# A two-layer decoder on one core: the score bias of the second cross-attention moved between engines, its outputs packed two heads to a slot, and the opening reordered

## The reference

```python
x = x + L0_attn(layernorm(x), ...)     # gated linear attention, cumulative sums over tokens
x = x + L0_xattn(layernorm(x), ctx)    # softmax cross-attention, keys beyond a length masked
x = x + L0_ffn(layernorm(x), ...)      # two rounds of routed experts, top 2 of 8
x = x + L1_attn(layernorm(x), ...)     # state-space scan, 16 states
x = x + L1_xattn(layernorm(x), ctx, fside, mask)   # softmax cross-attention with a bias
x = x + L1_ffn(layernorm(x), ...)      # quantised feed-forward, 128 -> 512 -> 128
```

```python
q = (query @ Wq.T + bq) * DH ** -0.5;  k = key @ Wk.T + bk;  v = value @ Wv.T + bv
scores = q @ k.T + attn_mask           # attn_mask (256, 256), the same for every batch and head
scores = where(key_padding_mask, -inf, scores)
out = softmax(scores) @ v              # then @ Wo.T + bo
```

## Time and profile before

| | us |
|---|---|
| median of 3 runs | 555.47 (551.81 to 556.1) |
| the profiled execution | 552.34 |
| its span in the profile | 550.6 |

### The profile page before, as it was taken

How to read it: one execution, slowest core, us unless ns; L and a number is a source line. 1 busy time by engine, 2 the same in 40 slices (tenths; PEclk the granted TensorE clock), 3 DMA queues, 4 the chain that set the end, 5 groups by cost and what they waited for, 6 DMA issues and landing times.

```text
span 550.6 us, 9218 instructions
## 1 busy us (share of the span) xinstructions
PE 469.6 (85%) x3087; PEld 276.5 (50%) x3095; DVE 440.8 (80%) x1164; ACT 279.0 (51%) x524; POOL 209.9 (38%) x190
## 2 busy tenths in 40 slices
PE   7789899999998989899989736545679999999866
PEld 6345666666555656566555302212224656666423
DVE  7798866677488557375875999999997789999897
ACT  3840356555544234354433546555530477777675
POOL 8834000000000403341701058999990245554061
PEclk9999999999999999999999956898789999999999
DMA  5510170000010211421200000000001000000001
GB/s 150 146 43 1 59 210 2 1 2 1 2 48 1 87 32 50 130 62 47 74 6 1 2 0 0 0 0 1 1 0 48 2 2 1 2 3 2 1 1 39
DMA packets 25392, 17.34 MB, mean 31 GB/s; under 512 B 2977, under 2 KB 24162, under 8 KB 25346
## 3 DMA queue, kind: packets, MB, share of 16 engines
q1 hardware_dynamic: 24322, 14.65, 9.3%
q0 software_dynamic: 1024, 2.10, 1.3%
HBM read 10.06 MB, written 5.51 MB: 28 GB/s over the span
## 4 chain that ended last, share of the span: by engine, by line
PE 39%; DVE 11%; POOL 11%; issue 5%; ACT 4%; POOLq 0%; DVEq 0%; ACTq 0%
PE PS L1346 7%; PE PS L814 5%; POOL E L2206 5%; PE PS L1460 4%; PE PS L1394 4%; POOL KSA L2198 3%; PE PS L859 3%; PE PS L876 3%; PE PS L1482 2%; POOL OT L2191 2%; PE PS L2085 1%; PE PS L1469 1%; PE PS L356 1%; PE PS L834 1%; PE PS L886 1%
## 5 line engine op out<-in xcount | busy, mean ns | idle before, releaser
L859 PE MATMUL PS<-QM,KP 32*128 32x256 f32 x512 | 91.9, 398 | 1.2 <-ACT E L1047 0.8
L814 PE MATMUL PS<-KP,QP 32*128 32x256 f32 x512 | 78.0, 400 | 0.5 <-ACT QP L1025 0.5
L1047 ACT ACTIVATE E<-PS 128x512 f32<-128x512 f32 x100 | 56.1, 595 | 35.0 <-PE PS L859 24.3
L2662 POOL DMA_INDIRECT sorted<-VA,slot_of x16 | 15.7, 980 | 145.3 <-DVE expert_at L1750 128.3
L859 PEld LDWEIGHTS PS<-QM,KP 32*128 32x128 f32 x512 | 60.6, 184 | 6.2 <-issue 4.8
L814 PEld LDWEIGHTS PS<-KP,QP 32*128 32x128 f32 x512 | 51.4, 184 | 14.5 <-issue 10.0
L1346 PE MATMUL PS<-XNT,KSA 128*128 128x512 f32 x128 | 58.6, 596 | 0.0
L1123 DVE CUSTOM_DVE_ANT_0 SCR<-PS,KSA 128x256 f32<-128x256 f32 x128 | 47.5, 420 | 9.1 <-PE PS L814 8.3
L356 PE MATMUL PS<-KSA,select 128*128 128x512 bf16 x60 | 23.4, 478 | 36.1 <-ACT KSA L2120 30.4
L1118 DVE TENSOR_REDUCE MXT<-PS 128x2 f32<-128x512 f32 x64 | 41.1, 686 | 14.4 <-PE PS L814 14.3
L2635 POOL TENSOR_TENSOR VA<-VA,KSA 128x512 f32<-128x512 f32 x28 | 35.2, 1275 | 37.4 <-ACT VA L1052 37.4
(11 more groups left out here) (343 smaller groups left out, 1033.3 us busy)
## 6 DMA issues: line engine op xcount, KB each, us to landing
KSA<-in_w SPq DMA_DIRECT2D x2, 1024.0 KB, 6.7
sorted<-zeros SPq DMA_DIRECT2D x2, 960.0 KB, 6.4
answers<-OT SPq DMA_DIRECT2D x14, 128.0 KB, 1.8
KSA<-in_w SPq DMA_DIRECT2D x2, 512.0 KB, 9.2
QP<-sorted SPq DMA_DIRECT2D x4, 256.0 KB, 3.1
QP<-sorted SPq DMA_DIRECT2D x2, 448.0 KB, 4.5
X<-in_x SPq DMA_DIRECT2D x2, 256.0 KB, 3.3
SCR<-in_ctxT SPq DMA_DIRECT2D x1, 512.0 KB, 6.3
```

What stands on the lines that cost most here:

```text
L814: ins = pe.matmul(score_bank(n, i)[:, q * S:(q + 1) * S], QP[rows(i), g, t:t + P], KP[rows(i), g, b * S:(b + 1) * S], start=True, stop=Tru ...
L859: ins = pe.matmul(o[:, kt * S:(kt + 1) * S], KP[rows(i), g, t:t + P], QM[rows(i), g, b * S:(b + 1) * S], start=True, stop=True, skip_group ...
L1047: act.activation(slot(m, j), drain_bank(L, m, j), ACT.Exp).then_inc(sig("exps"), 1)
```

## The change

It has three parts.

1. **Bias.** `LOOSE` becomes (0, 1): POOL biases items 0 and 1, DVE items 2 and 3. DVE's two adds of a quad are made together, after both items are computed: one instruction of 1024 columns where the two banks are neighbours, which holds for nine of the 14 quads (1, 2, 4, 5, 7, 8, 10, 11, 13), and two of 512 columns one after the other in the other five. ACT's late exponentials come in the quad's own round.
2. **Packed outputs, in both cross-attentions.** Quads 0 and 1 of a batch accumulate into the same columns, and so do quads 2 and 3: the value tile holds the odd quads' values 9 columns further on, with zeros elsewhere. So ACT's copy to OT has 256 columns in place of 512, and PE turns two blocks in place of four. The output weights of both cross-attentions are loaded in 16 DMAs in place of two, and the value tile is filled in more and smaller instructions.
3. **Opening.** POOL's fills of the value and query-weight tiles, and one of its mask operations, move from the front to behind the outer products of tiles 3 and 1. The projection of keys for the first cross-attention waits for features of batch 0, and ACT copies it after batch 1 (not batch 0). In `pair` the gate's exponential comes last. `turn_mixed` and `project_mixed` come one tile later on PE, and the gate of batch 3 comes after tile 5 on DVE.

```diff
@@ second cross-attention: who adds the bias
         def vector_bias(L, m, j):
-            return L == 1 and (m >= LOOSE_QUADS or j in (1, 2))
+            return L == 1 and (m >= LOOSE_QUADS or j not in LOOSE)
-        LOOSE = (0, 3)
+        LOOSE = (0, 1)
+        def neighbours(m):
+            return (HG * m + 2) % 3 < 2
...
+            def add_bias_pair(m):
+                dve.wait_ge(sig("shifted_scores"), I0 + HG * (m + 1))
...
+                if neighbours(m):
+                    first = 3 + (HG * m + 2) % 3
+                    o = PS[:, first:first + 2, :]
+                    ins = dve.tensor_tensor(o, o, BIASF.unsqueeze(1).to_broadcast([P, 2, HALF]), ALU.add)
+                else:
+                    for j in (2, 3):
+                        o = weight_bank(m, j)
+                        ins = dve.tensor_tensor(o, o, BIASF, ALU.add)
+                ins.then_inc(sig("biased"), 1)
...
                 for j in range(HG):
+                    if L == 1 and j == 3 and 0 <= k - LAG < LOOSE_QUADS:
+                        add_bias_pair(k - LAG)
                     if k < QUADS:
                         maximum(k, j)
-                    if 0 <= k - LAG < QUADS and vector_bias(L, k - LAG, j):
+                    if LOOSE_QUADS <= k - LAG < QUADS and vector_bias(L, k - LAG, j):
                         add_bias(k - LAG, j)
...
-                    if j == 0 and k > LAG and pool_bias(L, k - LAG - 1, 3):
-                        late_exps(k - LAG - 1, 3)
-                    if j == 1 and pool_bias(L, k - LAG, 0):
-                        late_exps(k - LAG, 0)
+                    if j in (1, 2) and pool_bias(L, k - LAG, j - 1):
+                        late_exps(k - LAG, j - 1)
@@ packed outputs
+                r, x = divmod(g, 2)
...
-                        ins = pe.matmul(bank(6)[rows(i), (g % 2) * S:(g % 2) * S + S], VX[:, QT * b + kt, HG * g + i, :],
-                                        slot(m, j)[:, kt * S:(kt + 1) * S], start=(kt == 0), stop=(kt == QT - 1),
-                                        skip_group_check=True)
+                        ins = pe.matmul(bank(6)[rows(i), r * S:(r + 1) * S], VX[:, QT * b + kt, HG * g + i, :],
+                                        slot(m, j)[:, kt * S:(kt + 1) * S], start=(kt == 0 and x == 0),
+                                        stop=(kt == QT - 1 and x == 1), skip_group_check=True)
...
-                for g in range(NG):
+                for r in range(2):
...
-                act.activation(OT[:, 2 * x:2 * x + 2, b * S:(b + 1) * S], bank(6).rearrange("p (g t) -> p g t", g=2),
-                               ACT.Copy).then_inc(sig("o_taken"), 1)
+                act.activation(OT[:, x, b * S:(b + 1) * S], bank(6)[:, x * S:(x + 1) * S], ACT.Copy)\
+                    .then_inc(sig("o_taken"), 1)
@@ output weights
-            for A in range(3):
-                load(woc[:, A, :], ...)
+            load(woc[:, 0, :], ...)
...
+            for A in (1, 2):
+                for k in range(2 * HG):
+                    r, i = divmod(k, HG)
+                    load(woc[16 * k:16 * k + 16, A, :],
+                         inp["w_out"][A][2 * r:2 * r + 2, 32 * i:32 * i + DH, :], "weights_in")
@@ opening
-            keys_project(pe, 0)
+            pe.wait_ge(sig("features"), 1)
+            pe.wait_ge(sig("self_taken"), 1)
+            keys_project(pe, FEATURE_BANK[0])
...
-                if b >= 2:
-                    read = (1, 3)[b - 2]
-                    pe.wait_ge(sig("features"), read)
-                    pe.wait_ge(sig("self_taken"), read)
+                if b == 2:
+                    pe.wait_ge(sig("keys"), 1)
+                if b == 3:
+                    pe.wait_ge(sig("features"), 3)
+                    pe.wait_ge(sig("self_taken"), 3)
...
-                if j == 4:
+                if j == 5:
                     turn_mixed(pe, 0)
-                if j == 5:
+                if j == 6:
                     project_mixed(pe, 0)
...
                 if b == 0:
                     entry_take(act, 0, 1)
-                    keys_take(act, 0)
                 if b == 1:
+                    keys_take(act, FEATURE_BANK[0])
                     keys_clear(act, range(NG))
...
-                    if b + 2 < B:
-                        feature(b + 2)
+                    if b == 0:
+                        feature(2)
+                    if b == 1:
+                        feature_soft(3)
                 if j == 5:
+                    feature_gate(3)
                     self_residual(dve, 0)
...
+                if j == 1:
+                    pool.tensor_scalar(NEGT, VMASK, -1.0, NEG_X0, ALU.add, ALU.mult).then_inc(sig("neg"), 1)
+                if j == 3:
+                    pool.memset(WP[:, :, :, :], 0.0).then_inc(sig("constants"), 1)
+                    value_frame(pool)
```

More of the change, by code:

```diff
@@ L71, in build @@
                    ("logits", 3): 6}
-        WEIGHTS = 16 * 16
+        WEIGHTS = 16 * 30
         def sig(name):
@@ L439, in context_values, with value_slots, take_values @@
             ins.then_inc(sig("vx_psum"), 1)
-        def take_values(act, dst, first_bank):
+        def value_slots(x):
+            return VX[:, :, :, :].rearrange("p j (r x i) c -> p (j r) x i c", r=2, x=2)[:, :, x, :,
+                                                                                        (DH + 1) * x:(DH + 1) * x + DH]
+        def take_values(act, first_bank):
             for half in range(2):
-                ins = act.activation(dst[:, 4 * half:4 * half + 4, :, 0:DH].rearrange("p j h e -> p (j h) e"),
-                                     bank(first_bank + half).rearrange("p (a e) -> p a e", e=DH), ACT.Copy)
+                src = bank(first_bank + half).rearrange("p (a x i e) -> p a x i e", x=2, i=HG, e=DH)
+                for x in range(2):
+                    ins = act.activation(value_slots(x)[:, 8 * half:8 * half + 8, :, :], src[:, :, x, :, :], ACT.Copy)
             return ins
@@ L463, in context_mask @@
             ch.link(ins)
-            pool.tensor_scalar(NEGT, VMASK, -1.0, NEG_X0, ALU.add, ALU.mult).then_inc(sig("neg"), 1)
             pool.wait_ge(sig("ctx_in"), 16)
@@ L467, in context_mask, with value_frame @@
             pool.tensor_tensor(CTM, CT, VMASK, ALU.mult).then_inc(sig("ctx_masked"), 1)
+        def value_frame(pool):
+            packed = VX[:, :, :, :].rearrange("p j (r x i) c -> p (j r) x i c", r=2, x=2)
+            for n in range(4):
+                js = slice(4 * n, 4 * n + 4)
+                pool.memset(packed[:, js, 0, :, DH + 1:32], 0.0)
+                pool.memset(packed[:, js, 1, :, 0:DH + 1], 0.0)
+                ins = pool.memset(packed[:, js, 1, :, 2 * DH + 2:32], 0.0)
+            ins.then_inc(sig("constants"), 1)
+            pool.memset(packed[:, :, 0, :, DH:DH + 1], 1.0)
+            pool.memset(packed[:, :, 1, :, 2 * DH + 1:2 * DH + 2], 1.0).then_inc(sig("constants"), 1)
         def neg_rows(eng, L):
@@ L612, in feature_soft @@
                 gate = GATE[:, js, :]
-                dve.wait_ge(sig("self_gate"), b + 1)
-                dve.tensor_scalar(gate, gate, 1e18, 1.0, ALU.min, ALU.add).then_inc(sig("gate_den"), 1)
                 dve.wait_ge(sig("self_sp"), b + 1)
@@ L617, in feature_soft @@
                 src = PS[:, FEATURE_BANK[b]:FEATURE_BANK[b] + QT, 0:2 * D]
+                dve.wait_ge(sig("self_taken"), b + 1)
                 dve.scalar_tensor_tensor(f, src, 0.0, f, ALU.max, ALU.add).then_inc(sig("features"), 1)
+                dve.tensor_scalar(gate, gate, 1e18, 1.0, ALU.min, ALU.add).then_inc(sig("gate_den"), 1)
             def feature_gate(b):
@@ L1269, in context_half_vector @@
             dve.wait_ge(sig("context_half"), half + 1)
-            dve.tensor_tensor(VX[:, 4 * half:4 * half + 4, :, 0:DH],
-                              bank(CONTEXT_BANK[half]).rearrange("p (j h e) -> p j h e", j=4, e=DH),
-                              brow[:, :].rearrange("p (h e) -> p h e", e=DH).unsqueeze(1).to_broadcast([P, 4, H, DH]),
-                              ALU.add).then_inc(sig(("half_read", "vx_ready")[half]), 1)
+            src = bank(CONTEXT_BANK[half]).rearrange("p (j r x i e) -> p j r x i e", j=4, r=2, x=2, e=DH)
+            row = brow[:, :].rearrange("p (r x i e) -> p r x i e", r=2, x=2, e=DH)
+            for x in range(2):
+                dst = value_slots(x).rearrange("p (j r) i e -> p j r i e", r=2)[:, 4 * half:4 * half + 4]
+                for r in range(2):
+                    ins = dve.tensor_tensor(dst[:, :, r, :, :], src[:, :, r, x, :, :],
+                                            row[:, r, x, :, :].unsqueeze(1).to_broadcast([P, 4, HG, DH]), ALU.add)
+            ins.then_inc(sig(("half_read", "vx_ready")[half]), 1)
         def tile_bank(i):
```

40 lines of the change are left out of this document (20 added, 20 removed).

## The result

Six runs of the changed kernel have a median of 559.05 us (557.19 to 561.31), six of the kernel before 553.03: a ratio of 1.0109, with a 95% interval of 1.0081 to 1.0137. The change costs 6 us. The forecast was 555.0 and no change; the time lies in its range of 549.5 to 560.5, outside the 552 to 558.5 that it gave for the forecast itself, and on the side it gave 0.16. The profiled execution of the changed kernel took 558.83 us, with a span of 557.1, against 552.34 and 550.6.

The account below looks back on a forecast made before the run. It took a loop of waits through the engines (4.78 us a round) as the bound; -2.6 + 0.2 - 1.8 + 5.9 - 0.4 = +1.3, on the 553.9 average, gave 555 us, range 549.5 to 560.5.

Parts of the forecast that it names:

- The loop through the add of item 2: Second cross-attention: item 2's exponential waits for both adds, lengthening the loop by 0.53 nine times and 0.61 five times; +5.9 us.
- Some of it is absorbed: Second cross-attention: VectorE's own queue covers part of the longer loop, taking 2 us off 7.9.
- Packed outputs: First cross-attention: `turn_out` rounds 0.22 shorter, six rounds and two tail turns, -1.8 us; value copies in four instructions, +0.2.
- The last tail: End of the second cross-attention: packed turns on the path save 0.2, ScalarE's shorter last copy 0.2; -0.4 us.
- The output weights: 16 SyncE loads in place of two cost 9.3 us more, under about 10 us of cover; cost 0.
- The opening: First stage: earlier batch 1 features and later `turn_mixed` bring the last tile's products from 57.66 to 55.1; -2.6 us.
- tile 2's products: Opening: these start at 32.7 and not 33.46, with batch 2's features at 27.3 on ScalarE; -0.8 us.
- The 1.80 at 47.09: Opening: VectorE's wait for tile 5's sums, held behind `turn_mixed`, goes when that comes later; -1.8 us.
- Rival C: Opening: GpSimd's fills hold VectorE's small operations by the shared-port lock, +1.9; sum +3.2, 557.1 us; chance 0.13.
- Rival A: Second cross-attention does not grow, as VectorE's queue decides everywhere; sum -5.3, 549.7 us; chance 0.2.
- Rival B: Loop absorbs nothing, residual rounds grow, opening gains nothing as fills delay batch 2; sum +6.5, 560.4 us; chance 0.12.

Follow-up runs that it names:

- run 7: Changed kernel with both adds still ahead of item 3's maximum, but each its own instruction with its own signal; 552.35 us, ratio 0.9998.
- run 6: Changed kernel with two adds one after the other in all 14 quads and no merged add; 560.07 us, ratio 1.0118.
- run 14: Changed kernel once more, without an edit; 559.96 us, ratio 1.012 to the kernel before.
- run 10: Packed outputs, reordered opening, old bias, idle products in the opening, idle turns beside output turns, GpSimd's query-weight fill back at the front; 550.32 us, ratio 0.9945.
- run 11: Changed kernel with a separate signal for each add and 12 more idle products in the opening; 551.34 us, ratio 0.9966.
- run 9: Changed kernel with the old bias, 12 more idle products in the opening and two idle turns beside each pair of output turns; 551.70 us, ratio 0.997.
- run 12: Kernel before with 6 more idle products before the turn of the entry norm in the opening; 552.62 us, ratio 0.9995.
- run 8: Changed kernel with the bias part undone and 12 more idle products in the opening; 550.97 us, ratio 0.9963.
- run 2: Kernel before with the reordered opening alone, value tile unpacked and filled by two memsets; 552.71 us, ratio 1.000.
- run 5: Changed kernel with idle products added in the opening and in the second cross-attention; 559.39 us, ratio 1.0113.
- run 1: Kernel before with the bias part of the change alone; 562.96 us, ratio 1.0177.

## Why the prediction was wrong

It forecast no change, and the change costs 6 us. Its main mechanism was right. What failed most is the opening's -2.6, of which -0.6 came; after it, what the loop's term left out, and the end of the span, which no term had. Step by step, in the frame of the profiled executions (+1.3 forecast, +6.5 found):

- **The loop through the add of item 2.** Right, and shown: run 7 against runs 6 and 14. The rows have 0.60 and 0.53 where 0.61 and 0.53 stood, plain rounds are 5.3 to 5.4. "Some of it is absorbed" was sized right as well: the wait for the second add is worth 80.87 - 74.75 = 6.1, against +5.9.
- **What the term left out.** What goes with the new split of items (+0.6), put nowhere in the sum, and two falls of the clock (+0.9). The +5.9 became +7.59.
- **Packed outputs.** 0.22 or 0.23 a round, as forecast; with the tail turns and the values -1.31 against -1.8 + 0.2. The last tail came to -0.36 against -0.4, but that is luck: run 10, packed, with the old split and filled turns, has 39.72 where 39.81 stood, so packing gives 0.1 there. The new split gives 0.5 (39.22 in run 11), and the late signal takes 0.2 back (39.45).
- **The output weights.** Right: SyncE issues the 16 loads in 10.31 us, and the key rows start at 26.00, as before (25.95).
- **The opening.** This step failed most: -2.6 forecast, -0.6 found. To tile 2's products it is +0.54 where -0.8 stood. With the key copy moved, tile 0 gains 1.74, but VectorE's L645 at 25.00, now beside GpSimd, takes 0.7 of it, the wait for the gate (0.93, was 0.34) 0.6, and the held L663 0.97 (from tile 1 to tile 2, 7.89, and 6.92 in run 9). From tile 2 to the last tile it is -2.20 where -1.8 stood, again a size met by luck. The 1.80 at 47.09 was read as a wait for `turn_mixed`; run 12, the same program up to there, has 0.42 of it, and the rest was TensorE at 1.2 GHz. At full clock this part gives 0.95 (22.95 in run 12, 22.00 in run 11). From the last tile to the first maximum it is +1.07 where 0 stood: 5.04, and 3.97 before and in run 9; that is the fall of the clock behind TensorE's wait of 3.46. At full clock the two openings start the cross-attention at 60.30 and 59.01 (runs 12 and 11), -1.3; in run 8, where L663 takes 1.17, it is 60.29, no gain.
- **Rival C, the lock.** It showed in part: L663 took 1.17 and ended at 30.04, where GpSimd's last fill ended at 30.00. The Trainium skill's rule ("SBUF — State Buffer", section "SBUF: two separate sides") has the later one wait for the other's whole instruction. The trace agrees in part: the fill that was running at 28.87 ended at 29.01, and L663 waited for five more; and the same operation beside the same fills took 0.18 in runs 9 and 11. In the 13 profiles with the changed opening it is longer in seven, by 0.1 to 1.0. L645 (another line number in runs 2 and 5) takes 1.18 or 1.19 in all 13, with GpSimd's outer products beside it, and 0.42 or 0.43 in the three with the old opening, where they had ended. So two operations were longer, not five, but together they cost 1.7 on the path, near the 1.9 that C gave.
- **The last issue.** 1.16 us at the very end were in nobody's sum. In the kernel before, one of SyncE's eight issues of the output takes 2.07 as well, but an earlier one, with nothing waiting. The last one is long (1.27 to 1.95) in seven of the 16 profiles, those of runs 9 and 11 among them, which are faster than the kernel before. No run ties it to the change, and what makes it long is not settled.
- **Rival A** is refuted by the rounds. Its time was also added up wrong: 553.9 - 5.3 is 548.6, not 549.7, and the bottom of the range leaned on it. **Rival B** had nearly the right time (560.4) and half of the reason: the opening gave next to nothing, but ScalarE came to batch 2 at 27.47, in time.

The errors were on the same side: 2.0 in the opening, 1.7 in the loop, 1.2 at the end, 0.3 in the packing.

## What to carry to other kernels

When two results are made by one instruction, or share one signal, look who waits for the first: here a merge that saved 0.08 us of VectorE delayed the next step of the loop by 0.53. A wait in a single profile should be checked against the granted clock of the engine that ends it before it is priced; 1.4 of 1.8 us were that. Here falls of the clock that came in one execution and not in another moved single stretches by 0.3 to 2.5 us, so parts worth 1 us are to be judged by the same events in both traces at full clock, and not by medians or by one profile.

## What was not expected of the hardware

The granted clock fell to 0.50 for 3 to 7 us in one execution and not in another. The changed kernel, run twice without an edit, has it at 445 to 448 and 455 to 458 in one profile and not in the other (run 14). Kernels with the same program in the stage differ in it as well: at 40 to 44 (before, not run 12) and at 506 to 510 (run 9, not run 10). In the opening the falls between 54 and 64 came with a wait of TensorE of 1.9 to 3.5 us, and with idle products in that wait none came; but the kernel before has the wait and no fall at 56 to 60, and run 9's windows just before its fall in the tail are full. The falls priced above cost between 0.3 us net (the first in the changed kernel's loop) and 2.5 us (the longer one in run 1). Why one comes and another doesn't stays open.
